# Reordered loads and small steps around the first convolution of a two-stage fused convolution kernel

## The chip, the cores and the metric

The kernel runs on one core of a Trainium2 chip. The metric is device time in microseconds (us), the median of several runs. A profiled execution gives the rows that are quoted; its times are counted from the start of its span. TensorE (PE) multiplies, VectorE (DVE) and ScalarE (ACT) work on elements, GpSimd (POOL) does the small sums of weights, and SyncE (SP) and ACT issue the transfers.

## What is computed

Two layers, each on a normalised copy of its input and added to it. Every channel of every image is normalised over its 64x64 pixels. Layer 0 is a 3x3 and a 5x5 convolution, mixed over nine shifts of the first by the table `wr`; the kernel folds all of it into one 5x5 convolution, with a correction for the picture's edges. Layer 1 convolves the products of each pixel's nine neighbours.

```python
def _L0_conv_ref(x, w3, b3, w5, b5, wr, br):
    y3 = lax.conv_general_dilated(x, w3, (1, 1), 'SAME', dimension_numbers=DN) + b3[None, :, None, None]
    y5 = lax.conv_general_dilated(x, w5, (1, 1), 'SAME', dimension_numbers=DN) + b5[None, :, None, None]
    P = jnp.pad(y3, ((0, 0), (0, 0), (1, 1), (1, 1)))
    shifts = [P[:, :, 2 - sw:2 - sw + H, 2 - sh:2 - sh + W] for sh in range(3) for sw in range(3)]
    stacked = jnp.stack([y5] + shifts, axis=2)
    return jnp.einsum('bcghw,cg->bchw', stacked, wr[:, :, 0, 0]) + br[None, :, None, None]
...
x = x + _L0_conv_ref(_gn(x), w3, b3, w5, b5, wr, br)
x = x + _L1_conv_ref(_gn(x), filters)
```

Here x is 8 images of 32 channels, w3 is 32x32x3x3, w5 is 32x32x5x5, wr is 32x10, and filters is 32x32x10x10, all float32.

## The kernel before

Four images of 32 channels fill the 128 partitions, so the eight images are two groups, 0 and 1. Everything is in program order on each engine; semaphores alone tie the engines together, and no scheduler moves anything. The change calls the first group "group one"; in the code and below it is group 0.

**Loads.** x of a group comes as four pieces of 512 KB (`load_raw`, L314), w3 and w5 as one copy for each of the four image rows (`by_image`, L321), wr as one broadcast transfer of 128 rows (L325). All of them are issued by SP and ACT in the first microseconds. SP then issues the biases and waits for the last piece of group 1 before it issues the filters of layer 1.

**Weights of layer 0.** DVE reorders w3 (`reorder_taps`, L620). ACT scales it nine times, once for each shift, with wr (`scale_shifts`, L564), and then w5 in two parts (L572). POOL adds the nine scaled copies one after the other into `folded` (L382), and between and behind them the two parts of w5 (`add_five`, L375) and the pair taps (L389, `pair_added`). DVE turns (transposes in 32x32 blocks, L624) the pair taps and, in `outer_taps`, the 25 taps. ACT copies parts of them (`copy_taps`, L487 to L491), and `middle_taps` on DVE makes the last ones (L649 to L655). Later POOL folds the weights of the edges (L405, L409) once half stream "left" is made, and then adds up the filters of layer 1 (L432 to L443).

**Group 0 of layer 0.** DVE takes the statistics of eight chunks (L741), finds scale and offset (L746 to L757, with ACT's square root at L477 in between), and writes 40 of 64 rows of the padded picture `plane` (L759), ACT the other 24 (L482). `halve` (L637) then makes half streams out of neighbouring columns: "total", "step", "left", "right", "far". TensorE starts with the product "next", straight from the plane with the pair taps, and goes on with "total" when its half stream and the middle taps are there, then with "step" and the others.

**Edges and hand over.** TensorE sums even and odd columns apart. `whole_and_cross`, `finish_even` and `finish_odd` (L663 to L673, DVE) put the parts together, `edges0` (L1101, L1109) computes corrections with TensorE once the odd half of group 0 is finished (`odd_ready`), `copy_edges` on ACT takes them out with the bias of the ring (`make_ring`, L679 to L694), and `spread` (L507, ACT) and `take_odd` (L814, DVE) copy the four images' halves back to `raw`. `finish_x1` (L825 to L829) adds the edges, and the statistics of layer 1 follow. Before its own group 1 work on "step" TensorE waits for `edges_copied`, and before "left" for `kept`, ACT's copy of the even sums (`keep_whole`, L497).

**Layer 1** is some 190 us of matmuls (L1007) on products that DVE makes (L879 and others), and the results leave at the end.

Of the kernel before, what the change touches and what calls it, by code (L numbers as in the profile page):

```python
# [6 lines left out]
GROUP = 4  # L7
# [91 lines left out]
def conv_kernel(nc, x, w3, b3, w5, b5, wr, br, filters, out):  # L99
# [12 lines left out]
    with ctx:  # L112
# [205 lines left out]
        def by_image(eng, to, weights, images, done):  # L318

            for r in images:  # L320
                eng.dma_start(to[32 * r:32 * r + 32, :], weights.rearrange("o c y x -> o (c y x)")).then_inc(done, 16)  # L321

        @block.sync
        def _(sp):
            sp.dma_start(wr_in[:, :], wr.rearrange("o g y x -> o (g y x)").partition_broadcast(GROUP))\  # L325
              .then_inc(branch_in, 16)
            by_image(sp, w3_in, w3, (0, 1), taps3_in)
            load_raw(sp, 0, range(PIECES))
            load_raw(sp, 1, range(PIECES))
            for n, v in enumerate((b3, b5, br)):  # L330
# [138 lines left out]
        def _(act):  # L469
            by_image(act, w3_in, w3, (2, 3), taps3_in)  # L470
            by_image(act, w5_in, w5, range(GROUP), taps5_in)
            act.wait_ge(zeroed, 1)
# [20 lines left out]
            def keep_whole(g):  # L493
                act.wait_ge(part_done, 4 * g + 1)
                if g == 1:
                    act.wait_ge(weight1_ready, 1)
                nc.scalar.activation(even_half(g), part_acc(0), ACT.Copy).then_inc(kept, 1)  # L497
# [85 lines left out]
            copy_edges(0, ROW_SIDES)  # L583
            copy_edges(0, COLUMN_SIDES)
            keep_whole(1)
            spread(0, 1, range(GROUP - 1))
            std(2)
# [22 lines left out]
        def _(dve):  # L610
# [133 lines left out]
            def normalise(phase):  # L744
                stage, g = divmod(phase, NG)
                step(nc.vector.bn_aggr(mean_var[:, :], stats[:, :, :].rearrange("p n s -> p (n s)")))  # L746
                nc.vector.tensor_scalar(norm[:, 0:1], mean_var[:, 1:2], GN_EPS, None, ALU.add).then_inc(var_ready, 1)
                if phase == 0:
                    dve.wait_ge(pair_added, 1)
                    turn(PAIR_AT, PAIR_AT + 5).then_inc(pair_ready, 1)  # L750
                dve.wait_ge(std_ready, phase + 1)
# [165 lines left out]
            dve.wait_ge(zeroed, 1 + NG)  # L917
            normalise(0)
            dve.wait_ge(padded, 4 * NG - 1)
            outer_taps()  # L920
            halve(0, "total")
            middle_taps(0)
# [10 lines left out]
            halve(1, "total")  # L933
            turn_edges()
            make_ring()
            finish_odd(0)
            halve(1, "step")
# [363 lines left out]
```

## Time and profile before

| | us |
|---|---|
| median of 3 runs | 302.14 (301.69 to 302.34) |
| span of the profiled execution | 300.4 |
| TensorE busy | 273.3 (91%) |
| VectorE busy | 252.8 (84%) |
| ScalarE busy | 87.6 (29%) |
| GpSimd busy | 29.0 (10%) |

For the profiled execution only its span is recorded, no time of its own; the median is 1.7 us above that span. The page shows TensorE nearly full from about 18 us on. Layer 0 lies between 0 and about 90 us and layer 1 behind it. The chain that ended last is TensorE for 71% of the span, DVE for 15% and ACT for 4%; most of what is not TensorE lies before 90 us and in the last 17 us.

### The profile page before, as it was taken

What the parts mean: (1) busy time and instruction counts of PE and PEld (TensorE: products, weight loads), DVE (VectorE), ACT (ScalarE), POOL (GpSimd) and SP (SyncE); (2) the same over time, 40 slices, a digit from 0 to 9 for tenths busy, and PEclk for the clock granted to TensorE, in tenths of its full rate; (3) what the DMA queues carried; (4) which work ended last, traced back from release to release, by engine and by line L of the source; (5) the groups of instructions that cost most, each with busy time, mean ns of one, the idle gap of its engine ahead of it and who ended that gap; (6) DMA issues with size and microseconds to landing.
All of it is one profiled execution on the core that took longest, in us unless ns stands there. A gap on an engine that the chain in (4) does not pass through costs nothing.

```text
span 300.4 us, 13567 instructions
## 1 busy us (share of the span) xinstructions
PE 273.3 (91%) x6464; PEld 130.6 (43%) x6464; DVE 252.8 (84%) x216; ACT 87.6 (29%) x135; POOL 29.0 (10%) x82
## 2 busy tenths in 40 slices
PE   0589999899999999999999999999999999999930
PEld 0224343344434433363546475344345446467310
DVE  1899899998999979799999999984999999970330
ACT  4532006979169789539000000004000000000000
POOL 7913920000110000000000000000000000000000
PEclk9999999999999999999999999999999999999995
DMA  6973000000000000000000000085000000000049
GB/s 190 382 203 82 4 2 3 2 5 2 2 2 4 4 2 4 2 2 3 4 2 4 2 4 4 2 171 115 2 2 4 2 2 4 2 4 4 2 91 189
DMA packets 19206, 11.45 MB, mean 38 GB/s; under 512 B 17744, under 2 KB 17872, under 8 KB 19024
## 3 DMA queue, kind: packets, MB, share of 16 engines
q1 hardware_dynamic: 14640, 9.06, 11.9%
q10 hardware_dynamic: 4512, 1.53, 2.2%
q8 instruction: 50, 0.82, 1.1%
q14 instruction: 4, 0.03, 0.0%
HBM read 6.40 MB, written 4.19 MB: 35 GB/s over the span
## 4 chain that ended last, share of the span: by engine, by line
PE 71%; DVE 15%; ACT 4%; issue 3%; DMA 2%; SPq 1%; DVEq 0%
PE acc L1007 63%; PE acc L1050 7%; ACT raw L507 3%; DMA raw<-in_x 2%; DVE stats L741 2%; DVE product L637 2%; DVE plane L759 2%; PE acc L1101 2%; DVE scaled L637 1%; DVE raw L801 1%; DVE product L872 1%; DVE product L663 1%; DVE product L669 1%; DVE arena L669 1%; DVE product L673 1%
## 5 line engine op out<-in xcount | busy, mean ns | idle before, releaser
L1007 PE MATMUL acc<-product,weight 32*32 32x512 f32 (+1 forms) x3072 | 126.8, 604 | 0.3 <-DVE product L872 0.3
L1007 PEld LDWEIGHTS acc<-product,weight 32*32 32x32 f32 (+1 forms) x3072 | 65.2, 110 | 59.4 <-issue 41.5
L879 DVE TENSOR_TENSOR product<-plane 128x4096 f32<-128x4096 f32 x19 | 83.3, 4430 | 0.1
L1007 PE MATMUL acc<-raw,weight 32*32 32x512 f32 (+1 forms) x960 | 45.4, 604 | 0.0
L1050 PE MATMUL acc<-product,middle 32*64 32x512 f32 (+1 forms) x576 | 30.2, 598 | 0.0
L1007 PEld LDWEIGHTS acc<-raw,weight 32*32 32x32 f32 (+1 forms) x960 | 20.7, 112 | 20.2 <-issue 15.7
L801 DVE TENSOR_TENSOR raw<-acc,arena 128x512 f32<-128x512 f32 x16 | 9.9, 683 | 16.7 <-issue 16.6
L1007 PE MATMUL acc<-product,arena 32*32 32x512 f32 (+1 forms) x448 | 22.2, 604 | 0.0
L879 DVE TENSOR_TENSOR raw<-plane 128x4096 f32<-128x4096 f32 x5 | 22.1, 4428 | 0.0
L741 DVE BATCH_NORM_STATS2 stats<-raw 128x6 f32<-128x512 f32 x32 | 19.7, 681 | 2.7 <-DMA raw<-in_x 2.6
L507 ACT ACTIVATE raw<-arena 32x512 f32<-32x512 f32 x32 | 21.8, 681 | 0.5
L537 ACT ACTIVATE arena<-acc 128x2048 f32<-128x2048 f32 x2 | 3.8, 1879 | 61.2 <-PE acc L1007 61.2
L637 DVE TENSOR_TENSOR product<-plane 128x2048 f32<-128x2048 f32 (+1 forms) x8 | 20.3, 2546 | 0.0
L507 ACT ACTIVATE raw<-product 32x512 f32<-32x512 f32 x28 | 19.0, 678 | 2.7 <-DVE product L669 2.3
L1050 PEld LDWEIGHTS acc<-product,middle 32*64 32x64 f32 (+1 forms) x576 | 11.1, 121 | 16.6 <-issue 15.7
L1120 PE MATMUL acc<-raw 32*64 32x512 f32 x64 | 5.9, 902 | 10.8 <-DMA raw<-in_x 10.8
L872 DVE TENSOR_TENSOR product<-product 128x2048 f32<-128x2048 f32 x6 | 13.6, 2286 | 2.0 <-PE acc L1007 2.0
L1007 PEld LDWEIGHTS acc<-product,arena 32*32 32x32 f32 (+1 forms) x448 | 8.6, 116 | 11.7 <-issue 9.4
L872 DVE TENSOR_TENSOR product<-raw 128x2048 f32<-128x2048 f32 x4 | 9.0, 2287 | 5.4 <-PE acc L1007 5.4
L1050 PE MATMUL acc<-plane,weight 32*64 32x512 f32 (+1 forms) x192 | 10.4, 635 | 1.2 <-DVE plane L759 1.2
L860 DVE TENSOR_TENSOR product<-plane 128x2048 f32<-128x2048 f32 x5 | 11.3, 2285 | 0.0
L1050 PE MATMUL acc<-scaled,weight 32*64 32x512 f32 (+1 forms) x192 | 10.7, 590 | 0.0
(121 smaller groups left out, 209.9 us busy)
## 6 DMA issues: line engine op xcount, KB each, us to landing
raw<-in_x SPq DMA_DIRECT2D x8, 512.0 KB, 8.3
out<-raw SPq DMA_DIRECT2D x24, 128.0 KB, 3.0
arena<-in_L_conv_filters SPq DMA_DIRECT2D x4, 400.0 KB, 6.9
out<-raw ACTq DMA_DIRECT2D x8, 128.0 KB, 4.7
arena<-in_L_conv_w ACTq DMA_DIRECT2D x4, 100.0 KB, 4.0
w_in<-in_L_conv_w ACTq DMA_DIRECT2D x2, 36.0 KB, 1.8
w_in<-in_L_conv_w SPq DMA_DIRECT2D x2, 36.0 KB, 2.2
b_in<-in_L_conv_b SPq DMA_DIRECT2D x2, 0.5 KB
```

The lines of the kernel that those rows point to most:

```text
L507: last = nc.scalar.activation(to[:, y:y + SIDE_ROWS - 1:2, odd:odd + W - 1:2], half[32 * s:32 * s + 32, CHUNK * r:CHUNK * r + CHUNK] .rear ...
L637: nc.vector.tensor_tensor(lines(buf, at, pitch)[:, 2:2 + H, 0:width], every_second(one), every_second(other), ALU.add if name == "total" e ...
L669: nc.vector.tensor_tensor(even_half(g), even_half(g), part_acc(0), ALU.add).then_inc(even_ready, 1)
L741: last = nc.vector.bn_stats(stats[:, n, :], raw[g][:, STAT * n:STAT * n + STAT])
L759: nc.vector.tensor_scalar(inner(g, 0, DVE_ROWS), raw_rows(g, 0, DVE_ROWS), mean_var[:, 0:1], norm[:, 5:6], ALU.subtract, ALU.mult).then_in ...
L801: nc.vector.tensor_tensor(view(result, 2 * CHUNK * r + odd, (W, CHUNK // HALF_W), (2, HALF_W)), acc[:, odd, r, :].rearrange("p (y x) -> p ...
L860: nc.vector.tensor_tensor(half_stream(g, u, half), plane_half(g, one), plane_half(g, other), ALU.add if (sides, half) == (0, 0) else ALU.s ...
L872: nc.vector.tensor_tensor(half_stream(g, u, half), half_stream(g, source, *one), half_stream(g, source, *other), ALU.add if (sides, half) ...
L879: nc.vector.tensor_tensor(both_halves(g, u), plane_halves(g), plane_halves(g, PRODUCTS[k][0] * PITCH + PRODUCTS[k][1]), ALU.mult)\
L1007: return nc.tensor.matmul(acc[32 * s:32 * (s + strips), j, r, :], weights[32 * r:32 * r + 32, t:t + strips, :] .rearrange("p t c -> p (t c ...
L1050: return nc.tensor.matmul(acc[32 * s:32 * (s + strips), odd, r, :], five[32 * r:32 * r + 32, t:t + strips, :].rearrange("p t c -> p (t c)" ...
L1101: last = nc.tensor.matmul(acc[32 * s:32 * s + 32, 1, side, 0:W], weight0[32 * r:32 * r + 32, EDGE_AT + 5 * EDGE_PLACE[side] + t + 2, :], p ...
```

## The change

Five things. SP issues the four pieces of x of group 0 first, then the four copies of w5, then group 1 of x. ACT issues all four copies of w3 and then wr. The pair taps are turned on DVE behind the plane, no longer between the variance and the square root's answer. On DVE the half stream "total" of group 0 now comes ahead of `outer_taps`, and `finish_odd(0)` ahead of `make_ring`. ACT copies the odd half of image 0 ahead of `keep_whole(1)` and the images 1 and 2 behind it.

```diff
@@ block.sync
-            sp.dma_start(wr_in[:, :], wr.rearrange("o g y x -> o (g y x)").partition_broadcast(GROUP))\
-              .then_inc(branch_in, 16)
-            by_image(sp, w3_in, w3, (0, 1), taps3_in)
             load_raw(sp, 0, range(PIECES))
+            by_image(sp, w5_in, w5, range(GROUP), taps5_in)
             load_raw(sp, 1, range(PIECES))
@@ block.scalar
-            by_image(act, w3_in, w3, (2, 3), taps3_in)
-            by_image(act, w5_in, w5, range(GROUP), taps5_in)
+            by_image(act, w3_in, w3, range(GROUP), taps3_in)
+            act.dma_start(wr_in[:, :], wr.rearrange("o g y x -> o (g y x)").partition_broadcast(GROUP))\
+               .then_inc(branch_in, 16)
@@ block.scalar
             copy_edges(0, COLUMN_SIDES)
+            spread(0, 1, (0,))
             keep_whole(1)
-            spread(0, 1, range(GROUP - 1))
+            spread(0, 1, range(1, GROUP - 1))
@@ def normalise(phase) of block.vector
-                if phase == 0:
-                    dve.wait_ge(pair_added, 1)
-                    turn(PAIR_AT, PAIR_AT + 5).then_inc(pair_ready, 1)
@@ block.vector
             normalise(0)
+            dve.wait_ge(pair_added, 1)
+            turn(PAIR_AT, PAIR_AT + 5).then_inc(pair_ready, 1)
             dve.wait_ge(padded, 4 * NG - 1)
+            halve(0, "total")
             outer_taps()
-            halve(0, "total")
             middle_taps(0)
@@ block.vector
             turn_edges()
+            finish_odd(0)
             make_ring()
-            finish_odd(0)
             halve(1, "step")
```

The queue of SP, from its start: before, the small table, half of w3 and all of x.

```order
L325 DMA wr_in<-in_L0_conv_wr 128x1x10
L321 DMA w3_in<-in_L0_conv_w3 32x288 x2
L314 DMA raw0<-in_x 128x1024 x4
L314 DMA raw1<-in_x 128x1024 x4
L331 DMA b_in<-in_L0_conv_b3 128x1x1
```

And in the changed kernel, where x of group 0 (`raw0`) leads and w5 (into `arena`) stands between the groups:

```order
L314 DMA raw0<-in_x 128x1024 x4
L321 DMA arena<-in_L0_conv_w5 32x800 x4
L314 DMA raw1<-in_x 128x1024 x4
L329 DMA b_in<-in_L0_conv_b3 128x1x1
L329 DMA b_in<-in_L0_conv_b5 128x1x1
```

x moved ahead by three issues; wr and w3 are gone from this queue, and those of w5 are new on it.

DVE at the start of group 0, from the first step of the scale on, before:

```order
L747 TENSOR_SCALAR norm<-mean_var 128x1 [waits chain]
L624 STREAM_TRANSPOSE weight0<-arena 128x160 [waits pair_added]
L752 RECIPROCAL norm<-norm 128x1 [waits std_ready]
L753 SCALAR_TENSOR_TENSOR norm<-norm 128x1 [waits chain]
L755 TENSOR_SCALAR norm<-norm 128x1 [waits chain]
L756 TENSOR_TENSOR norm<-norm 128x1 [waits chain]
L757 TENSOR_SCALAR norm<-mean_var,norm 128x1 [waits chain]
L759 TENSOR_SCALAR plane0<-raw0,mean_var,norm 128x40x64
L761 COPY means<-mean_var 128x1
L762 TENSOR_TENSOR norm<-norm 128x1
L624 STREAM_TRANSPOSE weight0<-arena 128x800 [waits columns_added,padded,chain]
L637 TENSOR_TENSOR product0<-plane0 128x2048 [waits plane_act,outer_turned]
```

And in the changed kernel, from the plane on (the lines of code are three lower there):

```order
L756 TENSOR_SCALAR plane0<-raw0,mean_var,norm 128x40x64
L758 COPY means<-mean_var 128x1
L759 TENSOR_TENSOR norm<-norm 128x1
L624 STREAM_TRANSPOSE weight0<-arena 128x160 [waits pair_added,chain]
L637 TENSOR_TENSOR product0<-plane0 128x2048 [waits plane_act,padded]
L624 STREAM_TRANSPOSE weight0<-arena 128x800 [waits columns_added]
L649 SCALAR_TENSOR_TENSOR middle0_0<-eye,norm,weight0 128x32 [waits taps_copied,outer_turned]
```

The turn of the pair taps (128x160) moved behind the plane, and "total" (L637) moved ahead of the turn of the 25 taps (128x800).

ACT around the copy of group 1's even sums (`arena<-acc`), before:

```order
L525 ACTIVATE edges<-acc,ring_bias 32x64 [waits ring_ready,edges_done]
L525 ACTIVATE edges<-acc,ring_bias 32x64 x7
L497 ACTIVATE arena<-acc 128x2048 [waits weight1_ready,part_done]
L507 ACTIVATE raw0<-product2 32x16x32 [waits odd_ready]
L507 ACTIVATE raw0<-product2 32x16x32 x11
```

And in the changed kernel:

```order
L524 ACTIVATE edges<-acc,ring_bias 32x64 x7
L506 ACTIVATE raw0<-product2 32x16x32 [waits odd_ready]
L506 ACTIVATE raw0<-product2 32x16x32 x3
L496 ACTIVATE arena<-acc 128x2048 [waits weight1_ready,part_done]
L506 ACTIVATE raw0<-product2 32x16x32 [waits odd_ready]
L506 ACTIVATE raw0<-product2 32x16x32 x7
```

Four of the twelve copies of the odd half moved ahead of the even sums' copy.

## Rows read from the trace of the kernel before

**Rows 1.** The page, first part: busy time of each engine, its share, its instructions

```profile
PE 273.3 (91%) x6464; PEld 130.6 (43%) x6464; DVE 252.8 (84%) x216; ACT 87.6 (29%) x135; POOL 29.0 (10%) x82
```

**Rows 2.** The chain that ended last: start us, length us, what

```profile
109.55 173.68 PE acc L1007 x3759
```

**Rows 3.** Timeline, SP's queue: start us, length of issuing us, queue, transfer

```profile
2.48 4.22 SPq L314 DMA_DIRECT2D raw<-in_x  x8
```

**Rows 4.** L321 on ACT's queue, issued 0.8 to 1.2 us: w3's first two copies

```profile
DMA to landing us min/median/max: 1.7/1.8/1.9
```

**Rows 5.** The same from 2.8 us on: the last two copies of w5

```profile
L321 ACTq DMA_DIRECT2D arena<-in_L_conv_w x2: 442/442/443, 2.8 to 3.2; - x2
...
DMA to landing us min/median/max: 4.7/5.5/6.4
```

**Rows 6.** L314, issued 2.4 to 3.0 us: first and second x piece, group 0

```profile
DMA to landing us min/median/max: 4.8/5.6/6.4
```

**Rows 7.** The same, 3.4 to 4.2 us: third and fourth piece

```profile
DMA to landing us min/median/max: 7.2/7.6/8.0
```

**Rows 8.** Timeline of DVE, start of group 0: start, length, instruction, idle before it

```profile
4.51 0.66 DVE L620 COPY w_taps<-w_in 128x288 f32<-128x288 f32 x1 [4.51 <-DMA w_in<-in_L_conv_w]
...
13.76 0.34 DVE L624 STREAM_TRANSPOSE weight<-arena 128x160 f32<-128x160 f32 x1
...
15.37 2.46 DVE L759 TENSOR_SCALAR plane<-raw,mean_var,norm 128x2560 f32<-128x2560 f32 x1
...
17.99 1.01 DVE L624 STREAM_TRANSPOSE weight<-arena 128x800 f32<-128x800 f32 x1
...
19.04 2.29 DVE L637 TENSOR_TENSOR product<-plane 128x2048 f32<-128x2048 f32 x1
...
22.37 2.35 DVE L637 TENSOR_TENSOR product<-plane 128x2112 f32<-128x2112 f32 x1
```

**Rows 9.** Groups by line before 20 us: busy us, mean ns of one, idle before

```profile
L741 DVE BATCH_NORM_STATS2 stats<-raw 128x6 f32<-128x512 f32 x8 | 5.1, 686 | 2.7 <-DMA raw<-in_x 2.6
```

**Rows 10.** Timeline of ACT and POOL in the same stretch

```profile
5.27 3.94 ACT L564 ACTIVATE scaled<-w_taps,wr_in 128x288 f32<-128x288 f32 x9
...
5.96 5.15 POOL L382 TENSOR_TENSOR arena<-arena,scaled 128x288 f32<-128x288 f32 x6 [0.93 <-ACT scaled L564]
...
9.63 2.00 ACT L572 ACTIVATE arena<-arena,wr_in 128x320 f32<-128x320 f32 x2 [0.41 <-DMA arena<-in_L_conv_w]
...
15.27 1.21 POOL L375 TENSOR_TENSOR arena<-arena 128x480 f32<-128x480 f32 x1
```

**Rows 11.** Instructions of L759, all four: ns min/median/max, first and last start

```profile
L759 DVE TENSOR_SCALAR plane<-raw,mean_var,norm x4: 1603/1605/2459, 15.4 to 131.8; 128x2560 f32<-128x2560 f32 x4
```

**Rows 12.** Timeline of DVE and POOL, 37 to 42 us

```profile
37.34 4.30 DVE L637 TENSOR_TENSOR product<-plane 128x2048 f32<-128x2048 f32 x1
...
38.59 0.90 POOL L443 TENSOR_TENSOR arena<-arena 128x192 f32<-128x192 f32 x1
```

**Rows 13.** Timeline of PE, "next" of group 0, and the edges

```profile
17.88 5.20 PE L1050 MATMUL acc<-plane,weight 32*64 32x512 f32 x96 [1.17 <-DVE plane L759]
...
57.62 0.96 PE L1101 MATMUL acc<-plane,weight 32*32 32x64 f32 x76 [1.36 <-DVE product L673]
```

**Rows 14.** Timeline of DVE, 52 to 74 us

```profile
52.84 0.97 DVE L624 STREAM_TRANSPOSE weight<-arena 128x768 f32<-128x768 f32 x1
...
55.19 2.28 DVE L673 TENSOR_TENSOR product<-product,acc 128x2048 f32<-128x2048 f32 x1
...
71.14 2.29 DVE L663 TENSOR_TENSOR arena<-arena,acc 128x2048 f32<-128x2048 f32 x1 [1.01 <-PE acc L1050]
```

**Rows 15.** Timeline of ACT, 62 to 77 us

```profile
62.71 2.54 ACT L525 ACTIVATE edges<-acc,ring_bias 32x64 f32<-32x64 f32 x8 [0.49 <-PE acc L1101]
66.15 1.88 ACT L497 ACTIVATE arena<-acc 128x2048 f32<-128x2048 f32 x1 [0.90 <-PE acc L1050]
68.05 8.38 ACT L507 ACTIVATE raw<-product 32x512 f32<-32x512 f32 x12
```

## The prediction

> **What bounds the kernel now.** I read the busy times first: TensorE is busy for 273.3 of 300.4 us and DVE for 252.8 [rows 1]. The chain of work says where that binds: from 109.55 us on it is one unbroken piece of matmuls of 173.68 us [rows 2]. None of the edits touches that part, so it moves as a block, and the question is only by how much its start moves. Before it I followed the chain back and then read the timeline of DVE, ACT, POOL and TensorE in two stretches.
>
> In the first stretch DVE is held by x: its eight statistics take 5.1 us and sit idle 2.7 us, for pieces of x [rows 9]. Then the plane is written from 15.37 to 17.83 us [rows 8], and TensorE, idle 1.17 us for it, starts "next" at 17.88 [rows 13]. Behind it DVE makes the 25 taps, "total" and the middle taps, and is done when "step" starts at 22.37 [rows 8]. TensorE is then near the end of "next" (5.20 us of work from 17.88), so both arrive together. In the second stretch TensorE waits 1.36 us for `finish_odd(0)` [rows 13], ACT waits 0.49 and 0.90 us for TensorE, and DVE 1.01 us [rows 14, 15].
>
> **The loads: what is won on x.** x of group 0 was issued from 2.48 us on [rows 3] and would be issued from 0.81, 1.67 us sooner. The third and fourth piece were issued at about 3.4 and 3.9 and landed 7.2 and 8.0 us later [rows 7], so at 10.6 and 11.9: a piece every 1.3 us. In the new order the first piece lands between 3.8 us (w3's first copy took 1.7 us [rows 4] from 0.81, plus one piece) and 5.6 us (the 4.8 of [rows 6]). The third lands at 6.4 to 8.2, the fourth at 7.7 to 9.5. That could give DVE up to 2.5 us.
>
> **The loads: what is lost on w3 and wr.** DVE cannot start the statistics until it has reordered w3, which before landed at 4.5 [rows 8], and ACT cannot scale without wr. How do small copies behave beside x? The last two copies of w5 were issued on ACT's queue at 2.8 and 3.2, just behind the first and second piece of x on the other queue (2.48 and 2.94). They landed 4.7 and 6.4 us later [rows 5], at 7.5 and 9.6. The pieces landed at 7.3 and 9.3 [rows 6]. So each copy, a fifth of a piece, landed 0.2 to 0.3 us behind the whole piece that was issued before it. With no x ahead a small copy takes 1.7 to 1.9 us [rows 4]. In the changed kernel w3's four copies are issued at about 0.8, 1.25, 1.7 and 2.1, each beside a piece of x, and wr at 2.6 behind all four. By these rows the last copy of w3 lands behind the third piece (I take 7.1; 6.7 to 9.8 if it is behind the third or the fourth) and wr behind the fourth (I take 8.4, range 7.0 to 9.8).
>
> The Trainium skill (DMA: Bandwidth & Descriptors, Queues, rings and completion order) says that each transfer engine alternates between the queues packet by packet, and that a completion is signalled only after every earlier write of that engine, across its queues. By that, a small load ends behind the piece of x in front of it; without it the sum would be that of rival B.
>
> From there: reorder at 7.1 (0.66), a small reduction (0.3, an estimate), eight statistics (5.1 [rows 9]) end at 13.2, and the variance is there some 0.5 later, at 13.7. Before, it was there at 13.76, where the pair taps were turned [rows 8]. **The lead of x is spent waiting for w3.** ACT's nine scalings start at 8.45 instead of 5.27 [rows 10], 3.2 us later. POOL's chain, 5.96 to 16.48 without a gap worth naming [rows 10], follows them, and ends at 19.7. w5 lands about 10 (fourth piece, wr, then four copies of a fifth of a piece each) and is not late for ACT, which is free at 12.4; w5's two scalings (2.0) end at 14.4.
>
> **DVE and POOL together.** The plane took 2.46 us here and 1.60 us three times later [rows 11]; only here was POOL adding (15.27 to 16.48). "right" took 4.30 us instead of 2.29, and ended 2.15 us after POOL's last addition of the filters at 39.49 [rows 12]. So a DVE operation of these kinds starts when POOL's additions leave room, and its own length comes on top.
>
> The Trainium skill (SBUF — State Buffer, SBUF: two separate sides) calls this an exclusive lock: whichever of the two starts first holds the shared ports for the whole instruction. The rows above show one direction, DVE waiting; that POOL is held in the same way no row shows clearly.
>
> Now `outer_taps` needs POOL's whole chain and, in the new order, "total" before it. I take both directions: POOL's end at 19.7, plus the plane's 1.6 (it has to fit in between POOL's additions), plus 2.3 for "total", gives a turn of the 25 taps at 23.6. Before, it was at 17.99. From its start come the turn (1.01), ACT's copy of 160 columns (0.45 with its signals, an estimate: turning as many takes DVE 0.34; "total" hid it before and it is open now) and the middle taps (22.37 less the 21.33 at which "total" ended, 1.0 to 1.1): 26.2, against 22.37. That is **+3.8 us**. TensorE starts "next" at about 19.5 to 20, because the pair taps (0.34 [rows 8], hidden beside the square root before) are turned behind the plane, and ends it at about 25, so it waits 1.2 us for the middle taps: no more is added there. Behind this, "step", "left" and POOL's edge and filter sums, which wait for "left" and hold "right" back [rows 12], shift by the same 3.8 us. With wr at 7.0 it is +2.4, with 9.8 it is +5.1.
>
> **The second stretch.** `make_ring` takes 1.4 us between 53.81 and 55.19 [rows 14]; ahead of it, the odd half is ready that much sooner and TensorE's 1.36 us are gone. The ring's bias then comes at 57.5, and ACT needs it only for the edges, which it copies from about 60.6 to 65.25, so that delay is covered. But TensorE may go on to "step" of group 1 only after this copying, and ACT comes to it straight from the 16 copies of the even half. It can save its idle 0.49 us [rows 15] and no more. So "step" starts 0.5 us sooner, and DVE at 71.14 [rows 14] gains 0.5 of its 1.01 us. The copy of image 0 (4 of 12 in 8.38, 2.8 us) delays the even sums' copy to 64.8 + 2.8 + 1.9 = 69.5 against 68.03. "Left" follows "step", whose last result DVE takes at 71.14, and after the gain at 70.6; the matmuls of "left" want the copy some tenths before that. So it is just covered, and if it is not, most of the 0.5 is lost. ACT's whole row ends at 75.0 instead of 76.43, ahead of DVE, whose three operations of 2.3 from 70.6 on end at 77.4 and are late next. I take **-0.5 us** for these edits, bounds 0 and -1.0.
>
> **Sum.** I find no slack behind these places that would take the shift up. 300.4 + 3.8 - 0.5 = 303.7 on the span, and with the 1.7 us between span and median **305.4 us**. Case A covers 303.5 (2.4 - 1.0) to 306.8 (5.1 - 0.4).
>
> **Rival B: small loads land as promptly as before.** For it: the first copies took 1.7 us [rows 4]. Against it: [rows 5, 6]. Then DVE's statistics end about 11, but ACT's w5 (issued behind x, landing 10 to 11.3) holds the root until 12.3 to 13.4, and POOL's chain ends at 16.5 to 17.6 as before. Plane and "total" have to fit around it: turn of the taps at 16.5 + 1.6 + 2.3 = 20.4 or later, so +0.6 to +1.6. Time 302.1 - 0.5 + 0.9 = 302.5, range 301.7 to 303.2.
>
> **Rival C, faster: small loads prompt, and POOL is not held by DVE.** For it: POOL's additions show no stretched length beside DVE's operations. Then the plane ends at about 15.5 to 16.5, POOL at 16.5, "total" at 18.2 to 19.3, and the middle taps come 0.5 to 1.6 us sooner; with neither held, 2.4. With the 0.5 this is 301.1 to 299.2, typical **300.8 us**. It decides at one point: the turn of the 25 taps must start before 19.8 us.
>
> **How the numbers follow.** Case A 0.62, B 0.20, C 0.18. This kernel can tell 0.2% (0.6 us) from no change. A is all slower. B I split into 0.13 within the band, 0.05 slower and 0.02 faster. C is 0.16 faster and 0.02 within. With 0.01 moved from A to within, faster 0.18, same 0.16, slower 0.66. The predicted time is A's, 305.4. For 8 in 10 the range takes all of A, B and the slow end of C: 301.2 to 306.8.
>
> **What would show each step.** DVE's reorder of w3 starting at 6.5 or later, and ACT's first scaling at 7 or later, show the waiting copies; both near 5 refute A. POOL's nine additions taking longer than the 0.86 us apiece of [rows 10] while the plane or "total" runs show the lock in the second direction. The turn of the 25 taps tells the cases apart: 22 to 25, 20.4 to 21.4, or before 19.8. The edges' matmuls should follow "next" of group 1 with no idle time, and ACT's copy of the edges' columns should start at once behind the rows'. I am wrong if wr or w3 overtakes x, or if DVE's later chain can absorb a late "left".

## The result, and the profile after

The changed kernel takes **309.5 us** (median of 4 runs, 308.7 to 310.0) against 302.2 for the kernel before: 1.023 times, 95% interval 1.021 to 1.025. The direction was forecast, but the time is 4.1 us above the 305.4 and 2.7 above the end of the range. The span of the profiled execution is 308.1 us, 7.7 more.

In the changed kernel many lines stand one to three lower in the code: the turn of the pair taps and of the 25 taps is still L624 and `halve` L637, but the plane is L756, ACT's scaling L563, POOL's additions L380 and L373, and layer 1 L1006. The chain that ended last, start and length:

```profile
2.68 11.22 DMA wr_in<-in_L_conv_wr
13.92 3.94 ACT scaled L563 x9
...
117.30 173.66 PE acc L1006 x3774
```

The unbroken piece of layer 1 is as long as in [rows 2] and starts 7.75 us later. It now hangs on `wr`, the smallest of the weight loads, which landed 11.2 us after it was issued. The queues, and then the landings of x of group 0 and of w3:

```profile
0.81 1.82 SPq L314 DMA_DIRECT2D raw<-in_x  x4
2.67 2.32 SPq L321 DMA_DIRECT2D arena<-in_L_conv_w  x4
```

```profile
DMA to landing us min/median/max: 4.2/6.1/8.0
```

```profile
DMA to landing us min/median/max: 3.5/5.2/6.2
```

x leads by the 1.67 us that were meant ([rows 3]: 2.48, now 0.81) and its fourth piece, issued at 2.2, landed at 10.2 where it had been 11.9 [rows 7]. But w3's last copy, issued at 2.2 too, landed 6.2 us later. [rows 4] had 1.7 to 1.9. DVE at the start of group 0 (start, length, instruction, idle time before it and what ended it):

```profile
8.47 0.67 DVE L620 COPY w_taps<-w_in 128x288 f32<-128x288 f32 x1 [8.47 <-DMA w_in<-in_L_conv_w]
...
19.81 0.16 DVE L749 RECIPROCAL norm<-norm 128x1 f32<-128x1 f32 x1 [4.93 <-ACT norm L476]
...
21.48 1.92 DVE L756 TENSOR_SCALAR plane<-raw,mean_var,norm 128x2560 f32<-128x2560 f32 x1
...
23.39 0.68 DVE L759 TENSOR_TENSOR norm<-norm 128x1 f32<-128x1 f32 x1
24.10 0.34 DVE L624 STREAM_TRANSPOSE weight<-arena 128x160 f32<-128x160 f32 x1
24.37 2.70 DVE L637 TENSOR_TENSOR product<-plane 128x2048 f32<-128x2048 f32 x1
28.16 1.01 DVE L624 STREAM_TRANSPOSE weight<-arena 128x800 f32<-128x800 f32 x1 [1.09 <-POOL arena L373]
...
30.77 4.56 DVE L637 TENSOR_TENSOR product<-plane 128x2112 f32<-128x2112 f32 x2
```

The reorder of w3 went from 4.51 [rows 8] to 8.47. The statistics then run without a stop and end at 14.3, and DVE nonetheless waits 4.9 us for the square root, because it stands on ACT behind the scaling, which waits for `wr`, and behind the scaling of w5. ACT and POOL:

```profile
13.92 3.94 ACT L563 ACTIVATE scaled<-w_taps,wr_in 128x288 f32<-128x288 f32 x9 [8.60 <-DMA wr_in<-in_L_conv_wr]
```

```profile
14.61 5.16 POOL L380 TENSOR_TENSOR arena<-arena,scaled 128x288 f32<-128x288 f32 x6 [9.58 <-ACT scaled L563]
...
21.26 3.66 POOL L380 TENSOR_TENSOR arena<-arena,scaled 128x288 f32<-128x288 f32 x3
25.00 3.13 POOL L373 TENSOR_TENSOR arena<-arena 128x480 f32<-128x480 f32 x1
```

The six additions take 5.16 us as in [rows 10]. The last three and the addition of w5, which now run beside the plane and "total", take 3.66 and 3.13 us; before they took 2.57 (the row below) and 1.21 [rows 10]. "Step" starts 8.4 us later than in [rows 8].

```profile
12.61 2.57 POOL L382 TENSOR_TENSOR arena<-arena,scaled 128x288 f32<-128x288 f32 x3
```

TensorE ran its warm-up matmuls to 12.8 us and was then idle for 8.84 us. In this gap, from about 18.2 us on, the clock granted to it fell to 0.50, the lower level of 1.2 GHz, and it came back to 1.00 at about 28.4. Its row of "next", and then a stretch inside that time (us, busy PE, PEld, DVE, ACT, POOL with counts, granted clock, DMA share, GB/s):

```profile
24.59 6.87 PE L1049 MATMUL acc<-plane,weight 32*64 32x512 f32 x96 [0.96 <-DVE weight L624]
```

```profile
18.60:28.20 9.60, 5.62 (x56) 1.75 (x64) 7.12 (x11) 2.85 (x4) 9.06 (x8) 0.50 0.72 155
```

In the second stretch the odd half is no longer waited for. The edges' matmuls follow without idle time, and neither ACT's copies nor DVE's first operation of group 1 have any (1.36, 0.49 and 1.01 us in [rows 13 to 15]):

```profile
64.55 1.05 PE L1100 MATMUL acc<-plane,weight 32*32 32x64 f32 x76
```

```profile
69.44 3.83 ACT L524 ACTIVATE edges<-acc,ring_bias 32x64 f32<-32x64 f32 x12
```

```profile
78.60 2.29 DVE L663 TENSOR_TENSOR arena<-arena,acc 128x2048 f32<-128x2048 f32 x1
```

Part of what TensorE gains ahead of the edges it waits for behind them, until ACT has copied them:

```profile
73.32 4.93 PE L1049 MATMUL acc<-product,middle 32*32 32x512 f32 x96 [0.66 <-ACT edges L524]
```

### The profile page after: what moved, and what is told of

Its sections match the earlier page's. It is cut to its first block, busy times and chain, and to the rows that moved or that the text cites. A ratio compares the mean times of both kernels' runs of the same rounds, so it can differ in the third digit from the quotient of the medians.

```text
span 308.1 us, 13568 instructions
## 1 busy us (share of the span) xinstructions
PE 275.1 (89%) x6464; PEld 131.2 (43%) x6464; DVE 253.6 (82%) x216; ACT 87.4 (28%) x135; POOL 32.0 (10%) x82
## 4 chain that ended last, share of the span: by engine, by line
PE 67%; DVE 12%; ACT 10%; DMA 4%; issue 3%; ACTq 1%; DVEq 0%
PE acc L1006 61%; ACT raw L506 6%; PE acc L1049 5%; DMA wr_in<-in_L_conv_wr 4%; DVE plane L756 2%; DVE stats L741 2%; DVE product L637 1%; DVE scaled L637 1%; ACT scaled L563 1%; ACT edges L524 1%; DVE raw L798 1%; PE acc L1100 1%; DVE product L869 1%; DVE product L669 1%; DVE product L663 1%
## 5 line engine op out<-in xcount | busy, mean ns | idle before, releaser
L1006 PE MATMUL acc<-product,weight 32*32 32x512 f32 (+1 forms) x3072 | 126.8, 604 | 0.3 <-DVE product L869 0.3
L1006 PEld LDWEIGHTS acc<-product,weight 32*32 32x32 f32 (+1 forms) x3072 | 65.3, 110 | 59.3 <-issue 41.6
L1006 PE MATMUL acc<-raw,weight 32*32 32x512 f32 (+1 forms) x960 | 45.3, 604 | 0.0
L1006 PEld LDWEIGHTS acc<-raw,weight 32*32 32x32 f32 (+1 forms) x960 | 20.7, 112 | 20.1 <-issue 15.7
L798 DVE TENSOR_TENSOR raw<-acc,arena 128x512 f32<-128x512 f32 x16 | 9.9, 679 | 16.6 <-issue 16.5
L1006 PE MATMUL acc<-product,arena 32*32 32x512 f32 (+1 forms) x448 | 22.2, 604 | 0.0
L637 DVE TENSOR_TENSOR product<-plane 128x2048 f32<-128x2048 f32 (+1 forms) x8 | 20.7, 2601 | 0.0
L1006 PEld LDWEIGHTS acc<-product,arena 32*32 32x32 f32 (+1 forms) x448 | 8.6, 116 | 11.7 <-issue 9.4
L1049 PE MATMUL acc<-plane,weight 32*64 32x512 f32 (+1 forms) x192 | 12.1, 712 | 1.0 <-DVE weight L624 1.0
L1049 PE MATMUL acc<-scaled,weight 32*64 32x512 f32 (+1 forms) x192 | 10.7, 590 | 0.0
```

The source lines that it names most:

```text
L637: nc.vector.tensor_tensor(lines(buf, at, pitch)[:, 2:2 + H, 0:width], every_second(one), every_second(other), ALU.add if name == "total" e ...
L798: nc.vector.tensor_tensor(view(result, 2 * CHUNK * r + odd, (W, CHUNK // HALF_W), (2, HALF_W)), acc[:, odd, r, :].rearrange("p (y x) -> p ...
L1006: return nc.tensor.matmul(acc[32 * s:32 * (s + strips), j, r, :], weights[32 * r:32 * r + 32, t:t + strips, :] .rearrange("p t c -> p (t c ...
L1049: return nc.tensor.matmul(acc[32 * s:32 * (s + strips), odd, r, :], five[32 * r:32 * r + 32, t:t + strips, :].rearrange("p t c -> p (t c)" ...
```

## The experiments

Two numbers are read from every trace: where "step" of group 0 starts on DVE, which closes the first stretch, and how long it is from there to the unbroken piece of layer 1. Ratios are to runs of the kernel before on the same chip.

| kernel | median us | ratio (95%) | "step" starts | from there to layer 1 |
|---|---|---|---|---|
| before | 302.2 | 1 | 22.37 | 87.18 |
| changed | 309.5 | 1.0232 (1.0212–1.0252) | 30.77 | 86.53 |
| old_loads | 303.6 | 1.0052 (1.0029–1.0074) | 23.25 | 87.37 |
| new_loads | 310.8 | 1.0279 (1.0255–1.0303) | 30.49 | 87.65 |
| wr_first | 306.9 | 1.0152 (1.0125–1.0180) | 28.05 | 85.50 |
| wr_rows | 306.9 | 1.0151 (1.0121–1.0181) | 27.58 | 86.33 |
| ring_odd | 302.4 | 0.9985 (0.9966–1.0004) | 22.81 | 86.87 |
| ring_only | 302.65 | 0.9998 (0.9980–1.0016) | 22.94 | 87.14 |
| odd_only | 302.3 | 0.9978 (0.9959–0.9997) | 22.89 | 87.58 |
| early_old | 302.9 | 1.0004 (0.9988–1.0020) | 23.52 | 86.81 |
| total_back | 303.5 | 1.0025 (1.0013–1.0037) | 23.06 | 88.41 |
| wr_act | 303.0 | 1.0017 (1.0002–1.0031) | 24.49 | 86.53 |
| early_best | 302.7 | 0.9997 (0.9983–1.0011) | 22.77 | 87.84 |
| warm | 307.9 | 1.0174 (1.0159–1.0189) | 30.02 | 85.17 |
| after_again | 309.3 | 1.0206 (1.0182–1.0230) | 30.61 | 86.58 |
| wr_rows_warm | 306.5 | 1.0122 (1.0100–1.0145) | 27.68 | 85.55 |

The last two columns come from one profiled execution of each kernel. Four kernels leave the first stretch as it was before or change in it only when the filters of layer 1 are issued (ring_odd, ring_only, odd_only, early_best), and their "step" starts at 22.77 to 22.94, not at 22.37. So about half a microsecond in that column is scatter, and the 22.37 lies at its early end.

### The change taken apart: loads, or the rest

old_loads is the changed kernel with the order of the loads of before; new_loads is the kernel before with the new order of loads alone.

```diff
 SP:  -load_raw(sp, 0), by_image(w5 x4), load_raw(sp, 1)
      +wr, by_image(w3, (0, 1)), load_raw(sp, 0), load_raw(sp, 1)
 ACT: -by_image(w3 x4), wr
      +by_image(w3, (2, 3)), by_image(w5 x4)
```

> The changed kernel with the old order of loads, all its other moves kept. Theory 1 (late wr and w3 carry the whole loss): the first scaling on ScalarE is back at about 5.3 us, and the time is 302.2 + 0.8 (pair turn and ScalarE's copy no longer hidden) - 0.7 (second stretch) = 302.3 us, between 301.5 and 303. Rival (the moves on VectorE cost most, by fighting with GpSimd): 305 us or more. Third possibility: the moves on VectorE cost nothing with loads on time, 301.5.

> The kernel before with the new order of loads and nothing else changed. Theory 1: wr lands at about 13.9 us as in the changed kernel; the pair turn now waits for GpSimd's pair sum at about 21.3 us, so 310 to 311 us, the changed kernel's 309.5 plus the 0.7 us that the second stretch gains. Rival (moves on VectorE cost most): 305 us or less.

The loads alone make the kernel 8.5 us slower, as expected; all but the loads 1.3 us (0.5%), which is 0.6 us above the range expected. The two don't add up to 7.3: with the late loads, "step" is late by 8.1 us with DVE's old order and by 8.4 with the new one, so DVE's moves cost 0.3 there. In old_loads they seem to cost 0.9 (23.25 against 22.37), but only 0.3 to 0.5 against the four kernels just named. And the second stretch is 1.1 us shorter in the changed kernel (86.53 against 87.65). With the old loads the turn of the 25 taps starts here:

```profile
20.66 1.00 DVE L625 STREAM_TRANSPOSE weight<-arena 128x800 f32<-128x800 f32 x1
```

That is close to the 20.4 of rival B. Its mechanism, "total" waited out in front of the turn, was right; only the loads that it supposed did not come.

### Why wr is so late

wr_first issues `wr` first on ACT's queue, ahead of w3. wr_rows leaves the order as it is, but loads `wr` by four copies of 32 rows.

```diff
-act.dma_start(wr_in[:, :], wr...partition_broadcast(GROUP))
+for r in range(GROUP):
+    act.dma_start(wr_in[32 * r:32 * r + 32, :], wr...)
```

> The changed kernel with wr issued ahead of the four copies of w3 on ScalarE's queue. Theory 1: wr lands by about 4 us, w3's last copy one piece of x later than its 8.4, at about 9.7 to 10.2; the first scaling goes from 13.9 to about 11 us, and the time to 306.5 us (305.7 to 307). If instead GpSimd's and VectorE's fight and not the late table set the time, the gain is under 1 us.

> The changed kernel with wr loaded as four copies of 32 rows at the same place, in place of one transfer of 128 rows. Theory 1a (the single transfer alternates several times with what stands on the other queue, because it is many small rows): each copy behaves like one of w3's; landing about 10 to 12 us, time 306 to 308 us. Theory 1b (it waits for the whole backlog of x whatever its form): landing 13.9, 309.5 us. A worse outcome: four copies wait for one x piece each, landing at 14 or later, 310 us or more.

ACT's scaling in wr_rows, and the reorder of w3 in wr_first:

```profile
10.74 3.94 ACT L563 ACTIVATE scaled<-w_taps,wr_in 128x288 f32<-128x288 f32 x9 [4.26 <-DMA wr_in<-in_L_conv_wr]
```

```profile
10.41 0.67 DVE L620 COPY w_taps<-w_in 128x288 f32<-128x288 f32 x1 [10.41 <-DMA w_in<-in_L_conv_w]
```

In wr_rows each of the four copies, though issued at 2.7 to 4.5 and so up to 1.8 us later than the one transfer, landed 5.9 to 6.2 us after its issue. Scaling starts 3.2 us sooner than in the changed kernel, "step" 3.2 us sooner, and the time is 2.6 us less. So it is worth 2.6 us of the loss that the 128 rows of 40 bytes go as one transfer and not as four.

The profile's counts of packets show where the 11.2 us went. `wr` stands behind w3 on ACT's queue, and w3's last copy landed at 8.4. From then on `wr` alone is left there, and in the five microseconds from 8 to 13 that queue moved 30, 27, 17, 16 and 24 packets, while SP's queue moved 71 to 122 in each. So `wr` was not held as a whole, its 128 small packets trickled for 5.5 us beside x and w5. In wr_rows the same packets went at 101 in the one microsecond from 8 to 9. The rows are of the same size in both, so that their smallness alone makes them slow is not shown; whether the number of rows in a transfer counts, or how a broadcast is dealt out to the 16 DMA engines, which the trace does not record, was not tested.

In wr_first `wr` is no longer last, w3 is (7.0 us to land), and the gain is the same, though in its trace 1.0 us comes from the stretch behind "step", where "right" went otherwise (below). That kernel says something more: its statistics start at 11.4, 2 us later than in the changed kernel, and it is still faster. DVE's statistics don't bound this stage, the chain through ACT's scaling and POOL does, and it starts when both w3 and `wr` are there.

wr_act is the change in its smallest form: the kernel before, with `wr` alone moved from the front of SP's queue to ACT's, between w3's two copies there and w5, and `make_ring` behind the odd half.

> The kernel before with one change: the load of wr goes from the front of SyncE's queue to ScalarE's, between the first two and the last two copies of w3, so that x is issued about 0.7 us sooner while nothing of w3 but its last two copies has a piece of x beside it. It is the change's idea in its smallest form. Theory (POOL's chain of additions sets the start of 'step', and it starts with ACT's scaling, not with x): x lands 0.5 to 0.7 us sooner, ACT's scaling starts no sooner than 5.3 and the time stays at 302.0 to 302.6; if wr falls behind a piece of x, scaling starts at 6 to 9 us and the time rises by as much less 0.5. Rival (x sets the start): 301.5.

```profile
7.54 3.94 ACT L564 ACTIVATE scaled<-w_taps,wr_in 128x288 f32<-128x288 f32 x9 [0.86 <-DMA wr_in<-in_L_conv_wr]
```

```profile
17.64 2.34 POOL L373 TENSOR_TENSOR arena<-arena 128x480 f32<-128x480 f32 x1
```

The same single transfer, issued at 1.73 and not at 2.68, and behind two copies of w3 and not four, lands 5.8 us later and not 11.2. Even so ACT's scaling starts 2.3 us later (5.27 in [rows 10]): it waits 0.86 us for `wr`, and the other 1.4 us are ACT's own issuing, which now ends at 5.15 and not at 3.68. "Step" starts 2.1 us later. Nor was x, issued 0.8 us sooner, all there sooner: the statistics ended at 13.7 us, before at 13.3. Against that the median is only 0.5 us higher (before: 302.6 on that chip) where 1.8 was expected. In the profile 0.65 us come back in the second stretch, and 1.5 are left in the span (301.9 against 300.4). Of these, 0.6 is that the profiled execution took 303.6 where the median is 303.0, and 0.4 that the kernel before had a median span of 300.8 on that chip and not 300.4.

### The second stretch

ring_odd is the kernel before with both moves, `finish_odd(0)` ahead of `make_ring` and image 0 ahead of `keep_whole(1)`; ring_only and odd_only have one each.

> The kernel before with only the moves of the second stretch: the odd half finished ahead of the ring, and image 0 of it copied ahead of the even sums. Theory: TensorE's 1.36 us wait before the edges goes, and 0.5 to 0.7 us is left at the end, since ScalarE's edge copies hold group 1: 301.6 us, ratio 0.998. Rival: all of the 1.36 us comes through, 300.9. Other rival: the early image copy delays the even sums and nothing is won, 302.2.

> The kernel before with only the odd half finished ahead of the ring. Theory: this carries the gain of the second stretch. ScalarE's copies of group 0's odd half are then followed through as before, with the even sums copied about 1 us sooner: 301.6 us, as with both moves. If the image copy is what fills ScalarE's idle 0.9 us, this alone gives 301.9 or more.

> The kernel before with only image 0's odd half copied ahead of the even sums. Without the ring moved TensorE's edges are as late as before, so the even sums' copy comes at about 70 instead of 68 us on ScalarE. Theory: group 1's product left waits up to 0.3 us for it and the time is 302.2 to 302.6. A gain of 0.5 us or more would say that ScalarE's row of copies was the bound by itself.

They took 302.4, 302.65 and 302.3 us beside 302.8 for the kernel before: ratios 0.9985 (0.9966 to 1.0004), 0.9998 (0.9980 to 1.0016) and 0.9978 (0.9959 to 0.9997). ring_odd's stretch is 0.3 us shorter than before's, the changed kernel's 0.65. So the forecast -0.5 us fits within what can be measured, though of these three only odd_only is told from no change, and barely. How the gain is shared out between the two moves is not settled: odd_only, from which nothing was expected, did as well as both, and the trace doesn't say by what, since its stretch is 0.4 us longer than before's. ring_only shows why one move alone need not pay. ACT's copy of the even sums then waits for DVE, which turns the filters first:

```profile
66.78 1.88 ACT L497 ACTIVATE arena<-acc 128x2048 f32<-128x2048 f32 x1 [1.19 <-DVE weight L703]
```

### A hole in TensorE's work

In old_loads TensorE stops in the middle of "step" of group 0, with no wait that the trace shows. The weight loads stop for 1.64 us and the matmuls, whose ends the profile only models, for 0.76; the weight loads, with the idle time before them:

```profile
27.75 0.23 PEld L1050 LDWEIGHTS acc<-product,middle 32*64 32x64 f32 x15 [1.64 <-issue]
```

My theory was that its next instructions are fetched late because the filters of layer 1 are loading (they are issued at 17.3). early_old is old_loads with the filters issued three us sooner, without SP's wait for x; early_best is ring_odd with that same edit.

```diff
-sp.wait_ge(piece_in[1][PIECES - 1], 16)
```

> The changed kernel with the old order of loads, as old_loads (303.6 us), and the filters issued right behind the biases instead of behind the last x piece's landing. In old_loads TensorE stands still for 1.6 us at 26.1 to 27.8 us and waits for nothing that the trace shows, while the filters' transfer ends. Theory: what is missing is a block of TensorE's own program, queued behind the filters; with the filters landed by about 21 us the hole goes and the time is about 302.9. Rival: the hole belongs to something else and stays, 303.6.

> The kernel before with the two moves of the second stretch (ring behind the odd half, image 0 copied ahead of the even sums) and the filters' load issued without waiting for the last piece of x of group 1. The two moves alone took 302.4 where before took 302.8. Theory (the two moves are worth 0.4 to 0.7 us, and the filters' load in front of the late waits of TensorE takes away a hole of up to 1.6 us that some runs show at 27 us): 301.6 to 302.0, with no idle time over 0.3 us on TensorE at 26 to 29 us. Rival (the hole is filled by waiting elsewhere, DVE's odd half at 52 us is what counts): no less than with the two moves alone, 302.4.

early_old took 302.9 us, ratio 1.0004 (0.9988 to 1.0020), and of the hole 0.44 us were left. That looked like proof, and early_best undid it: the filters leave at 14.5, the time is 302.7 us (ratio 0.9997), and the hole is there.

```profile
27.50 0.23 PEld L1050 LDWEIGHTS acc<-product,middle 32*64 32x64 f32 x15 [1.50 <-issue]
```

So the theory falls, and what makes the hole stays open; it lies at the same instruction in six of the kernels (0.85 to 1.64 us between weight loads) and not in the profiled execution of before. It also costs less than it is long. Where TensorE is late, DVE's "right" comes later as well, and finds POOL nearly done with its sums of the filters (below): in early_best the first result of "step" is taken 2.4 us later than before, yet "right" ends at 42.0 against 41.6. No version beats the kernel before by more than the 0.2% that can be told.

### DVE's order in the first stretch

total_back is old_loads with the 25 taps turned ahead of "total" again; the pair taps stay behind the plane.

> The changed kernel with the loads in the order of before, and with the outer taps turned ahead of 'total' again (the pair taps stay behind the plane, both moves of the second stretch stay). With the loads of before alone the outer taps were turned at 20.66 and 'step' started at 23.25, where before it started at 22.37. Theory (DVE and POOL hold each other for whichever operation starts first, and 'total' in front of the turn holds back both POOL's last addition and ACT's copy of the taps): the outer turn starts at 18.0 to 18.6, 'step' at 22.3 to 22.8, time 0.5 to 0.9 us below that of the old loads alone, about 302.9. Rival (the 0.9 us comes from the pair turn in the chain of the plane): 'step' stays at 23.0 or later and the time within 0.3 us of 303.6.

```profile
18.47 1.24 DVE L625 STREAM_TRANSPOSE weight<-arena 128x160 f32<-128x160 f32 x2
```

The two turns run one behind the other, ending at 19.7; "step" starts at 23.06, 0.2 us before that of old_loads and not the 0.5 to 0.9 that I expected. The rival had 23.0 or later and a time near 303.6, and that is what came (303.5). The time decides less than it seems: as ratios to the kernel before, 1.0025 against 1.0052, total_back is better by up to 0.8 us, with intervals that overlap. What differs from before lies ahead of the plane: two operations on 128x1 between the root and the plane took 0.79 and 1.05 us where before they took 0.22 and 0.45, and the plane starts at 16.70 and runs 1.60, where it started at 15.37 and ran 2.46 [rows 8]. It ends at 18.3 against 17.8, in both cases 1.3 to 1.8 us behind the end of POOL's last addition at 16.5. DVE is held either before the plane or in it. That is not the work of the moved turn: in the four kernels with the first stretch of before, the second of these operations takes 1.05 us too and the plane starts at 16.63 to 16.80.

### TensorE's low clock

warm is the changed kernel with `warm_up(13)` in the place of `warm_up(3)`, so that TensorE has matmuls until its first real work. after_again is the changed kernel itself, and wr_rows_warm is wr_rows with the longer warm-up.

> The changed kernel with 208 instead of 48 warm-up matmuls, so that TensorE is busy up to about 20 us instead of 12.8 before its first real work at 21.6. It asks whether the granted clock of 0.50 that TensorE showed from about 18.6 to 28.2 us in the changed kernel is a part of the miss. Theory (the clock costs next to nothing, since 'step' of group 0 waits for DVE's middle taps and not for 'next'): 'next' shrinks from 6.6 to about 5 us, 'step' still starts within 0.3 us of 30.8, time 309.2 to 309.6. Rival (the clock is a term of its own): 'step' starts 1 us or more sooner, time 308.5 or less.

> The changed kernel itself once more, beside the kernel that follows and the kernel before, so that the effect of longer warm-up can be read in one sitting. With 208 warm-up matmuls the changed kernel took 307.95 us against its 309.52, and in the two profiled executions wr landed 0.75 us sooner, 'step' of group 0 was finished another 0.5 us sooner, and DVE's 'right' was not held by POOL (2.29 instead of 4.33 us). Theory 'clock and lock': the changed kernel takes 309.2 to 309.8 again, its 'right' takes 4 us or more and wr lands at 13.5 or later, so that the gain is not a thing of the day. Rival 'landing': wr lands at 13.1 and the time is 308.5 or less, and then the gain of the longer warm-up is 0.5 us or less.

> The changed kernel with wr as four copies of 32 rows, which took 306.93 us, and with 208 warm-up matmuls. With the four copies alone TensorE, at a granted clock of 0.50 from 21 to 26 us, needed 7.75 us for 'next' and started 'step' 1.3 us behind DVE's middle taps (28.91 against 27.58), and 'right' was held until POOL had ended its additions at 44.67 and took 3.39 us. Theory (the low clock costs only where 'next' is late for the middle taps, as here): 'next' takes 5.2 us, 'step' of group 0 is finished 1.0 to 1.3 us sooner. If 'right' is still held until POOL's end, the gain is given back there and the time stays at 306.6 to 307.1; if DVE gets its turn 3.4 us after POOL's first of the twelve additions, as in the two runs where it did, the time is 305.2 to 305.8. Rival (the clock is worth its whole length wherever it ends): 305.4 whatever 'right' does.

The granted clock stays at 1.00 in warm and "next" takes 5.17 us and not 6.87. I had expected 0.3 us at most, and the kernel is faster by 0.3% (beside after_again, where the intervals overlap) to 0.6% (beside the first runs), 1.0 to 1.7 us. after_again took 309.3 us, as expected, so the changed kernel's time is no accident of its first runs. From DVE's start of "step" to its first result there are 9.94 us in warm, 10.42 in the changed kernel, 10.16 in after_again and 10.44 before. So 0.2 to 0.5 us come from TensorE. The rest of what the two profiles differ by I put down to two other things: `wr` landed 0.8 us sooner in that execution, and at "right" something else happened. DVE and POOL in warm:

```profile
44.49 2.29 DVE L637 TENSOR_TENSOR product<-plane 128x2048 f32<-128x2048 f32 x1
```

```profile
41.05 10.17 POOL L441 TENSOR_TENSOR arena<-arena 128x192 f32<-128x192 f32 x12
```

and in after_again:

```profile
45.30 4.56 DVE L637 TENSOR_TENSOR product<-plane 128x2048 f32<-128x2048 f32 x1
```

```profile
41.66 6.05 POOL L441 TENSOR_TENSOR arena<-arena 128x192 f32<-128x192 f32 x12
```

When DVE comes to "right", POOL is at its twelve sums of the filters. Either POOL keeps the way, does them in 6.05 us, and DVE's operation ends 2.15 us behind the last one; or DVE gets through in 2.29 us and POOL's sums take 10.2. The second is 2 us better, since nobody waits for the filters then. It fell out so in wr_first, warm and wr_rows_warm, with DVE coming 3.43, 3.44 and 3.79 us after POOL's first sum, and the other way in after_again, the changed kernel and before, at 3.64, 3.88 and 3.90. The time of coming does not decide it alone. In the other ten kernels DVE came 4.1 us or more behind POOL's first sum, and POOL's sums took 6.04 to 6.07 us in all of them.

In wr_rows_warm "next" takes 5.13 us and not 7.75, and the first result of "step" comes 10.34 us behind DVE's start and not 11.33. This is the 1.0 us expected, since in wr_rows the slow "next" ended 1.3 us behind the middle taps. "Right" was free too, for which 305.2 to 305.8 was expected. It took 306.5, ratio 1.0122 against 1.0151: about 0.9 us better, with intervals that overlap. In the trace 1.2 us of gain are still there at 51 us; at 75 us, where DVE waits 0.87 us for TensorE, 0.4 are left. What is won ahead of the edges is partly waited away behind them.

## Why the prediction was right or wrong

**The path: right.** Layer 1 moved as one block, and the shift is that of its start. Nothing behind the two stretches took it up.

**The lead of x is spent waiting for w3: right, a little too small.** w3's last copy landed at 8.4; I took 7.1, with bounds 6.7 to 9.8. x's fourth piece came at 10.2, where 7.7 to 9.5 was forecast, and DVE did not wait for it. The statistics ended at 14.3 and not 13.2, and that mattered to nobody.

**wr lands at 8.4, range 7.0 to 9.8: wrong.** This is the step that failed. It landed at 13.9, so ACT's scaling started 8.65 us later than before and not 3.2. I had priced `wr` from the w5 copies of [rows 5] as a small load that ends just behind the large piece in front of it. The 8.4 is when w3's last copy landed, behind which `wr` stood; its own 128 packets then took another 5.5 us beside the other queue, and for these the sum had nothing. It ended behind the fourth piece (10.2), behind all of w5 (the last of it issued at 4.6, landed 7.5 later), which was issued beside it on the other queue, and behind the first piece of group 1 (13.1). Those priced copies are 32 rows of 3 KB; `wr` is 128 rows of 40 bytes. With four copies of 32 rows it fits the forecast's kind of price (5.9 to 6.2 us from issue, ready at 10.7).

The Trainium skill (DMA: Bandwidth & Descriptors, Queues, rings and completion order) has the transfer engines alternating between the queues packet by packet. The landings and the packet counts here agree: both queues move packets all the time, and a transfer of 128 small ones pays for the other queue's packets more than once. Why the same 128 rows go faster as four transfers it leaves open, and so do the runs.

**DVE and POOL hold each other: right, priced somewhat high.** Both signs named for it are there: POOL's last addition took 3.13 us and not 1.21 while "total" ran, and DVE's plane and "total" came to 1.92 and 2.70. From ACT's first scaling to the turn of the 25 taps I had 15.15 us (8.45 to 23.6), and there were 14.24 (13.92 to 28.16). Holding cost 3.0 us behind POOL's own end and not 3.9.

The Trainium skill (SBUF — State Buffer, SBUF: two separate sides) calls it a lock that lasts a whole instruction, whichever engine comes first. [rows 11, 12] showed DVE waiting; the trace after now shows POOL waiting as well. One thing goes beyond that rule: at "right" of the changed kernel DVE did not get in after one instruction of POOL's, but waited while five of the twelve sums ran (45.72 to 47.90).

**From the turn to "step": right.** 2.6 us forecast, 2.61 measured, with ACT's copy open at 0.47.

**The sum of the first stretch** therefore errs by 5.47 us (13.92 less 8.45) and, the other way, by 0.91: "step" started at 30.77 where 26.2 was forecast, +8.4 and not +3.8. That is the whole miss of the span (308.1 against 303.7), with 0.15 us back from the second stretch.

**Second stretch, -0.5 us: right.** -0.65 in the changed kernel; no idle time before the edges, at ACT's edges or at DVE's first operation of group 1. The bound is the one forecast too: TensorE waits 0.66 us for ACT's copies of the edges.

**TensorE's clock: not priced.** I had "next" from 19.8 to 25 at full clock. It ran from 24.59 to 31.2, which was hidden but for 0.5 us, since "step" had to wait for the middle taps to 30.8. Against the kernel before it cost nothing, so it is no part of the miss. With `wr` 3 us sooner in wr_rows it becomes a term of 1 us; in wr_first, where the clock was back at 1.00 by 25 us, it is none (9.95 us from DVE's "step" to its first result).

## What to carry to other kernels

A load is priced by its form as well as by its place in the queue: one transfer of 128 rows of 40 bytes, issued behind the small loads and beside large ones, came 11.2 us after its issue, each of four transfers of 32 such rows about 6 us, and at the front of a queue no engine waited for it. Before a large load is moved to the front, ask which small one starts the longest chain of dependent work, and leave that one where it is: here POOL's twelve additions hung on `wr`, while DVE had several us of slack with x. And when two engines share a way, look at the pair in both directions, since a move that puts a DVE operation ahead of a turn also puts it into POOL's sums.

## What the runs showed of the hardware that I had not expected

- The same broadcast of `wr` took 5.8 us when issued at 1.73 us and 11.2 us when issued at 2.68 us, behind all of x's four pieces and of w3's four copies. In the second case it moved at 16 to 30 packets a microsecond, and cut into four transfers at up to 101.
- Of two engines that come upon each other at "right", either can get its way: 2.29 and 10.2 us, or 4.3 to 4.6 and 6.05. It was worth 2 us at that place, and may be one reason why single edits moved these kernels by more or by less than their own size; that was not tested by itself.
- Operations on a single column are held too: the one of L759 took 0.68 us beside POOL and 0.15 without.
- In a gap of 8.8 us without matmuls TensorE's granted clock fell to 0.50 and stayed there from about 18.2 to 28.4 us. It also fell to 0.50 with gaps of 7.4 us (after_again) and 4.6 us (wr_rows). With the longer warm-up, and with the gap of 1.2 us in the kernel before, it stayed at 1.00.
- A stop of up to 1.6 us between TensorE's weight loads, and up to 0.76 us between its matmuls, with nothing waited for, at the same instruction in six kernels. Loading the filters sooner shortened it to 0.44 us in one kernel and not in the other.
